# Forming the attention values for 256 queries at a time, with shorter rings of probabilities

## The reference, cut to what matters

```python
q, k, v = (xs @ W.T + b for W, b in ((Wq, bq), (Wk, bk), (Wv, bv)))   # (8, 1024, 512), in 8 heads of 64
energy = jnp.einsum('nhqd,nhkd->nhqk', q, k)
attn = jax.nn.softmax(energy / np.sqrt(HEAD_DIM), axis=3)
out = jnp.einsum('nhql,nhld->nhqd', attn, v)
out = out.reshape(N, -1, Cc) @ Wo.T + bo
```

## Time and profile before

| | us |
|---|---|
| median of 3 runs | 2842.52 |
| lowest and highest | 2835.03, 2848.33 |
| profiled execution | 2847.47 |
| span of its profile | 2845.7 |

### The profile page before, as it was taken

The page is one execution under the profiler, slowest core; times in us unless marked ns, Lnnn a source line. Parts: engine busy times, 40 slices in busy tenths (PEclk is TensorE's granted clock), DMA queues, the critical chain, the costliest instruction groups (busy, mean ns, idle before and its releaser), DMA issues. The chain is left out here.

```text
span 2845.7 us, 37765 instructions
## 1 busy us (share of the span) xinstructions
PE 2572.5 (90%) x13344; PEld 2093.9 (74%) x13344; DVE 1917.9 (67%) x3508; ACT 1736.0 (61%) x3048; POOL 900.3 (32%) x804
## 2 busy tenths in 40 slices
PE   4999898998899988999889989899898998999976
PEld 3788767887578766887768877688766887678864
DVE  4678656786477863877648776477765877567753
ACT  3677436774377734777347763477635775467732
POOL 0244303443044430443304433144421444124420
PEclk9999999999999998999999999999999999999997
DMA  6224103331113212222122231222402323032300
GB/s 234 60 72 121 74 17 85 78 104 74 51 52 88 93 74 61 60 71 93 75 61 71 71 112 44 63 69 74 152 1 72 78 63 145 1 89 71 93 30 30
DMA packets 79975, 215.54 MB, mean 76 GB/s; under 512 B 9968, under 2 KB 10256, under 8 KB 74000
## 3 DMA queue, kind: packets, MB, share of 16 engines
q1 hardware_dynamic: 79760, 212.77, 24.6%
HBM read 103.68 MB, written 25.17 MB: 45 GB/s over the span
## 5 line engine op out<-in xcount | busy, mean ns | idle before, releaser
L1036 POOL TENSOR_SCALAR PR_loop<-PR_loop,rinv_loop 128x1024 f32<-128x1024 f32 x448 | 503.7, 1124 | 1249.0 <-DVE rinv_loop L1004 1248.8
L1029 DVE TENSOR_TENSOR PL_loop<-pT_loop,PH_loop 128x512 fp32r<-128x512 f32 x896 | 576.0, 684 | 254.0 <-ACT PH_loop L984 252.4
L984 ACT ACTIVATE PH_loop<-pT_loop 128x512 fp32r<-128x512 f32 x896 | 487.2, 596 | 296.7 <-PE pT_loop L909 292.6
L999 DVE TENSOR_REDUCE nmax_loop<-pS_loop 128x1 f32<-128x1024 f32 x448 | 545.0, 1216 | 123.7 <-PE pS_loop L899 118.6
L954 ACT ACTIVATE PR_loop<-pS_loop,nmax_loop 128x1024 f32<-128x1024 f32 x448 | 501.2, 1119 | 24.8 <-DVE nmax_loop L999 22.5
L909 PE MATMUL pT_loop<-ident,PR_loop 128*128 128x128 f32 x3584 | 467.7, 273 | 18.1 <-POOL PR_loop L1036 18.1
L909 PEld LDWEIGHTS pT_loop<-ident,PR_loop 128*128 128x128 f32 x3584 | 415.2, 141 | 93.2 <-POOL PR_loop L1036 40.9
L898 PE MATMUL pS_loop<-KHL,QS 128*128 128x512 f32 x896 | 368.4, 411 | 58.5 <-issue 53.2
L930 PE MATMUL pO_loop<-PH_loop,VS 128*128 128x512 f32 x896 | 360.0, 402 | 21.5 <-DVE OT L1020 20.2
L931 PE MATMUL pO_loop<-PL_loop,VS 128*128 128x512 f32 x896 | 357.5, 399 | 0.0
L899 PE MATMUL pS_loop<-KHL,QS 128*128 128x512 f32 x896 | 356.8, 398 | 0.0
(11 more groups left out here) (284 smaller groups left out, 4065.5 us busy)
## 6 DMA issues: line engine op xcount, KB each, us to landing
KHL<-HL_loop SPq DMA_DIRECT2D x168, 256.0 KB, 3.6
WQ<-wqk_split SPq DMA_DIRECT2D x64, 512.0 KB, 5.8
QS<-HL_loop SPq DMA_DIRECT2D x168, 128.0 KB, 3.1
X<-in_x SPq DMA_DIRECT2D x32, 512.0 KB, 9.4
WO<-wo_split SPq DMA_DIRECT2D x16, 1024.0 KB, 6.8
X_loop<-in_x SPq DMA_DIRECT2D x28, 512.0 KB, 5.5
KHL<-wv_split SPq DMA_DIRECT2D x14, 1024.0 KB, 9.8
out<-X_loop SPq DMA_DIRECT2D x14, 1024.0 KB, 7.9
```

What stands on the lines that cost most here:

```text
L984: act.activation(PH[ck % 2][:, 4 * half:4 * half + 4, (g % 4) * P:(g % 4 + 1) * P], pT[half][:, :].rearrange("p (k n) -> p k n", k=4), ACT ...
L999: dve.tensor_reduce(nmax[:, g:g + 1], pS[g % 2][:, :], AX.X, ALU.max, negate=True)\
L1029: dve.tensor_tensor(PL[ck % 2][:, ks, qs], pT[half][:, :].rearrange("p (k n) -> p k n", k=4), f32(PH[ck % 2][:, ks, qs]), ALU.subtract).th ...
L1036: pool.tensor_scalar(PR[g % 2][:, :], PR[g % 2][:, :], rinv[:, g:g + 1], 1.0, ALU.mult, ALU.mult)\
```

## The change

A group is now 256 queries (`GQ`), two steps. `PH`, `PL` and `OB` hold 256 queries; the rings stay rings of two groups. `values(ck)` does all its 16 matmuls, of 256 columns now, in one step: in the odd steps from g = 3 on. `OB` and `OT` come in every even step, for 256 columns. The loop on PE ends after step 65, in place of 67. As both `PH` buffers now lie where `X1` was, the wait for `b_store` moves from g == 4 to g == 0.

```diff
+GQ = 256
-        PH = [sb(f"PH{i}", [P, ST, 512], F32R) for i in (1, 0)][::-1]
-        PL = [sb(f"PL{i}", [P, ST, 512], F32R) for i in range(2)]
+        PH = [sb(f"PH{i}", [P, ST, GQ], F32R) for i in (1, 0)][::-1]
+        PL = [sb(f"PL{i}", [P, ST, GQ], F32R) for i in range(2)]
-        OB = [sb(f"OB{i}", [D, 512]) for i in range(2)]
+        OB = [sb(f"OB{i}", [D, GQ]) for i in range(2)]
...
-            def values(ck, part):
-                h = ck // 2
-                if part[0] == 0:
-                    pe.wait_ge(S["a_lo"], 8 * (ck + 1))
-                    if ck >= 1:
-                        pe.wait_ge(S["a_o"], ck)
-                for kb in range(*part):
+            def values(ck):
+                h = ck // 4
+                pe.wait_ge(S["a_lo"], 4 * (ck + 1))
+                if ck >= 1:
+                    pe.wait_ge(S["a_o"], ck)
+                for kb in range(ST):
                     v = VS[:, kb, h, :]
-                    pe.matmul(pO[:, :], v, PH[ck % 2][:, kb, :], start=(kb == 0), stop=False)
-                    mm = pe.matmul(pO[:, :], v, PL[ck % 2][:, kb, :], start=False, stop=(kb == ST - 1))
+                    pe.matmul(pO[:, 0:GQ], v, PH[ck % 2][:, kb, :], start=(kb == 0), stop=False)
+                    mm = pe.matmul(pO[:, 0:GQ], v, PL[ck % 2][:, kb, :], start=False, stop=(kb == ST - 1))
...
-            for g in range(STEPS + 4):
+            for g in range(STEPS + 2):
                 if g + 2 < STEPS:
                     scores(g + 2)
-                if g >= 4 and g % 4 > 0:
-                    values(g // 4 - 1, ((0, 3), (3, 6), (6, 8))[g % 4 - 1])
+                if g >= 3 and g % 2 == 1:
+                    values((g - 3) // 2)
...
-                if g >= 8 and g % 4 == 0:
-                    ck = g // 4 - 2
+                if g >= 4 and g % 2 == 0 and g <= STEPS + 2:
+                    ck = (g - 4) // 2
...
-                    elif g == 4:
+                    elif g == 0:
                         act.wait_ge(S["b_store"], 16 * NCH)
```

More of the change, by code:

```diff
@@ L920, in project @@
                     mm.then_inc(S["a_proj"], 1)
-            def values(ck, part):
-                h = ck // 2
-                if part[0] == 0:
-                    pe.wait_ge(S["a_lo"], 8 * (ck + 1))
-                    if ck >= 1:
-                        pe.wait_ge(S["a_o"], ck)
-                for kb in range(*part):
+            def values(ck):
[4 more added lines that the diff above has]
+                for kb in range(ST):
                     v = VS[:, kb, h, :]
-                    pe.matmul(pO[:, :], v, PH[ck % 2][:, kb, :], start=(kb == 0), stop=False)
-                    mm = pe.matmul(pO[:, :], v, PL[ck % 2][:, kb, :], start=False, stop=(kb == ST - 1))
-                if part[1] == ST:
-                    mm.then_inc(S["a_pv"], 1)
+                    pe.matmul(pO[:, 0:GQ], v, PH[ck % 2][:, kb, :], start=(kb == 0), stop=False)
+                    mm = pe.matmul(pO[:, 0:GQ], v, PL[ck % 2][:, kb, :], start=False, stop=(kb == ST - 1))
+                mm.then_inc(S["a_pv"], 1)
             scores(0)
@@ L965, in _ @@
                         act.wait_ge(S["a_o"], ck - 1)
-                    act.activation(OB[ck % 2][:, :], pO[D:P, :], ACT.Identity,
-                                   bias=b_v[D:P, ck // 2:ck // 2 + 1]).then_inc(S["a_obot"], 1)
+                    act.activation(OB[ck % 2][:, :], pO[D:P, 0:GQ], ACT.Identity,
+                                   bias=b_v[D:P, ck // 4:ck // 4 + 1]).then_inc(S["a_obot"], 1)
                 if copying(g):
@@ L976, in _ @@
                 if g < STEPS:
-                    ck = g // 4
+                    ck = g // 2
                     if ck >= 2:
                         act.wait_ge(S["a_pv"], ck - 1)
-                    elif g == 4:
+                    elif g == 0:
                         act.wait_ge(S["b_store"], 16 * NCH)
@@ L983, in _ @@
                         act.wait_ge(S["a_tr"], 2 * g + half + 1)
-                        act.activation(PH[ck % 2][:, 4 * half:4 * half + 4, (g % 4) * P:(g % 4 + 1) * P],
+                        act.activation(PH[ck % 2][:, 4 * half:4 * half + 4, (g % 2) * P:(g % 2 + 1) * P],
                                        pT[half][:, :].rearrange("p (k n) -> p k n", k=4), ACT.Copy)\
@@ L1013, in _ @@
                     recip(g + 1)
-                if g >= 8 and g % 4 == 0:
-                    ck = g // 4 - 2
-                    hh, n = divmod(ck, 2)
+                if g >= 4 and g % 2 == 0 and g <= STEPS + 2:
+                    ck = (g - 4) // 2
+                    hh, n, j = ck // 4, ck // 2 % 2, 2 * (ck % 2)
                     dve.wait_ge(S["a_obot"], ck + 1)
-                    dve.tensor_tensor(OT[n * D:(n + 1) * D, :, hh * P:(hh + 1) * P],
-                                      pO[0:D, :].rearrange("d (j m) -> d j m", j=CT),
-                                      OB[ck % 2][:, :].rearrange("d (j m) -> d j m", j=CT), ALU.add).then_inc(S["a_o"], 1)
+                    dve.tensor_tensor(OT[n * D:(n + 1) * D, j:j + 2, hh * P:(hh + 1) * P],
+                                      pO[0:D, 0:GQ].rearrange("d (j m) -> d j m", j=2),
+                                      OB[ck % 2][:, :].rearrange("d (j m) -> d j m", j=2), ALU.add).then_inc(S["a_o"], 1)
                 if g < STEPS:
-                    ck = g // 4
+                    ck = g // 2
                     for half in range(2):
                         ks = slice(4 * half, 4 * half + 4)
-                        qs = slice((g % 4) * P, (g % 4 + 1) * P)
+                        qs = slice((g % 2) * P, (g % 2 + 1) * P)
                         dve.wait_ge(S["a_hi"], 2 * g + half + 1)
```

## The result

The changed kernel takes 2981.7 us (median of four runs) against 2838.8 before: a ratio of 1.050 with a 95% interval of 1.046 to 1.053. Slower, as forecast, but by 143 us and not by 62, and above the range of 2865 to 2955. Span against span it is 2982.2 for 2845.7, 136.5 us.

A forecast was written before the change was run, and what follows sets the result against it. PE was taken as the bound, 100% busy between turns 11 and 50. Terms 1.6 + 4.7 + 3.8 - 2.3 = 7.8 us per image, 62 for eight, gave 2910 us profiled, 2905 us median; range 2865 to 2955.

The forecast's parts named there:

- The direction, and why: Whole kernel: slower by 7.8 us per image, as bunched values leave long and short intervals; chance of slower 0.90.
- The price of the matmul: Value matmuls on PE: one of 256 columns costs 0.118 us, inside a band of 0.114 to 0.121.
- the extra 14 ns: Value matmuls: 512 columns cost 14 ns above their cycles; if owed per matmul, 256 columns cost 0.121 us.
- The stretches ahead of turn 11 and behind turn 50, and the end: Both ends of an image: +3.8 us before turn 11, +4.7 behind turn 50, -2.3 behind turn 63.
- 4.02 and 2.38: Behind turn 50: intervals with values take 4.02 us, waiting for `OT`; those without take 2.38.
- the three terms named (0.26, 1.8 and 0.53): Behind turn 63: `OT` 0.26 us shorter, value matmuls 3.4 us for 5.2, `OB` and `OT` 0.84 for 1.37.
- The middle stretch: Turns 11 to 50: nine periods +2.3 us, three further intervals -0.7, net +1.6 us per image.
- the 4.15 us interval that follows: Projection stretch: this interval hides the under 0.5 us by which the added `OB` delays `PH` on ACT.
- The wait for the store: Ahead of the first `PH`: stores land over 8 us before that write, so the moved wait costs nothing.
- the load is hidden: Rival for value matmuls: load and matmul not fully overlapping, distance 0.14 to 0.19 us, 2995 to near 3200 us; chance 0.12.
- the clock stays at 1.00: Rival: PE idling twice per pair of steps lowers the clock, 3 to 6 us per image, 2930 to 2955 us; chance 0.09.
- long intervals of 3.6: Rival: `OT` comes no later than the scores' end, long intervals 3.6 us, short 2.2; 2828 us, chance 0.07.

## Why the prediction was wrong, point by point

*The direction, and why*: right. Smaller groups put 16 matmuls into one interval and none into the next, and the intervals without values fall under what the other engines need.

*The price of the matmul*, taken as 0.118 out of 0.109 to 0.19: measured 0.120. The load of the stationary operand hides beside 256 columns. The reading that the extra 14 ns belong to a matmul and not to its columns (0.121) was the nearest. The formula for an isolated matmul in the Trainium skill, "TensorE: Matmul & The Clock Gate", section "Back-to-back issue gap", which gives 109 ns, is 11 ns below this trace.

*The stretches ahead of turn 11 and behind turn 50, and the end*: right in that `OT` holds the long intervals, and within 0.3 us each, but this closeness is partly luck. Long intervals of 4.1 to 4.24 and short ones of 2.17 stand where 4.02 and 2.38 were put; the pair is 6.3 for 6.40. The 2.38 was no property of the ring `pT`: the row at 615.70 names POOL as what PE waited for there. In the changed kernel such a turn waits for `PL`, and comes at 2.17. At the end the three terms named (0.26, 1.8 and 0.53) add up to 2.6 and not to the 2.3 written. They measured 0.18, 1.71 and 0.48, together 2.4.

*The middle stretch*, the term of +1.6 us: this step failed; it measured +11.6. The prediction tested the shortened interval against the transposes' own ring (`pT`) and found 2.25 us a little short, which the runs do not bear out (the interval is 2.26, its plain PE work); it did not ask the same of the other thing that PE does behind the early turn, the projection. It even had the late `QK` on ACT, but followed that delay only to `PH` ("hidden by the 4.15 us interval that follows") and not to the engine that waits for `QK` itself, PE, for which it frees the one bank. Nine waits of 1.1 us in each of eight images make 79 us; the middle stretch missed its forecast by 10.0 us per image, 80 in all. The remaining differences of a period nearly cancel: the interval with the wait has 0.1 more than the wait explains, the one from turn 12 to 13 is 4.86 for 4.82, and the one from 13 to 14 is 2.26 for 2.38. Removing the wait does not give back all of it: with the projection a step later the middle stretch fell by 6.9 us per image, 55 in all, since the `OT` gate then holds the interval at 4.00 to 4.14 although two matmuls have left it.

*The wait for the store*: forecast as nothing. ACT does wait for it once, ahead of the first `PH` of the eighth image:

```profile
ACT PH_last L983 <- DMA out<-X_loop: 1.2, 1, 1.2
```

It costs PE nothing there: turn 1 follows turn 0 by 2.76 us, as in image 1. The images of the loop have no such wait.

*The rivals*: the load is hidden (0.120 us from start to start), the clock stays at 1.00 between turns 0 and 63 of image 1, and `OT` does not come early enough for long intervals of 3.6. None of them was the cause of the miss. The case that another buffer runs out, here the one bank `pJ`, was not among them.

## What to carry to other kernels

When work is bunched, some interval becomes shorter: list every wait that the engine reaches earlier by it, with its present margin (here 1.04 us at the one bank `pJ`), and compare with the shift. The comparison has to include what arrives later by the same change (here 1.36 us earlier on PE and 0.63 later on ACT). A delay that is found must be followed to every engine that waits for that result, not only down its own queue. And look where a sum such as `OB` and `OT` stands in its queues: a step earlier it cost 0.14 us a period where PE was full, and saved 0.3 us in the stretch where PE was waiting.

## What was not expected of the hardware

A float32r matmul of 256 columns with a new stationary operand each time costs 0.120 us, while its load is recorded with 0.19 us, more than the distance: a record is no occupancy. `OB` of 256 columns took 0.47 us, not half of 0.68, and `OT` 0.41. In the kernels with `OB` and `OT` early throughout, PE idled at most 1.6 us behind turn 63 and the granted clock of the end stayed at 1.00. PE idled 2.2 us there in the kernel before, where the clock of the end read 0.83, and in the changed one, where it read 0.80; from the second on, the matmuls of the changed kernel's end came 0.213 us apart.
